# A second table of levels 1 to 8 for the key tiles one behind the diagonal, and no product of the high table in that level unit

## What is computed

```python
def _level_structure(t, num_levels):
    """level 0: s == t; level l>=1: t - s in [2^(l-1), 2^l). Clamped to num_levels-1."""
...
q = (x @ Wq.T).reshape(b, t, H, S); k = ...; v = ...            # H = 8, S = 128
g = -jax.nn.softplus(x @ Wg.T + bg)
lam = jax.nn.softplus((x @ Wdl.T).reshape(b, t, H, LV) + Lparam[None, None])   # LV = 12
G = jnp.cumsum(g, axis=1)
scores = jnp.einsum('bthd,bshd->bhts', q, k) * scale
decay = jnp.exp(jnp.where(mask, Gh[:, :, :, None] - Gh[:, :, None, :], -jnp.inf))
lamw = jnp.einsum('bthl,tsl->bhts', lam, lvl_oh)                # the weight of the level of t - s
y = jnp.einsum('bhts,bshd->bthd', scores * decay * lamw, v)
out = y @ Wo.T + x            # then a layer norm, a residual,
...                           # and a layer of 8 experts of which the best 2 are summed
```

## Time and profile before

| | before |
|---|---|
| three runs | 1454.74, 1455.56, 1457.22 us; median 1455.56 |
| span of the profiled execution, first to last instruction | 1454.1 us (no own time is given with it; it lies 0.6 below the lowest run) |
| busy: TensorE, VectorE, ScalarE, GpSimd | 95%, 72%, 81%, 64% of the span |
| mean granted TensorE clock | 0.991 of full speed |
| instructions | 30713, of them 10470 matmuls |
| transfer packets | 256341, 44.03 MB |

### The profile page before, as it was taken

One profiled execution on the slowest core, in us unless ns is written; L12 is line 12 of the kernel. 1 busy time (PEld: TensorE's weight loads), 2 busy tenths in 40 slices (PEclk: granted clock), 3 DMA queues, 4 the chain that ended last, 5 costly groups with the idle time before them and its releaser, 6 DMA issues.

```text
span 1454.1 us, 30713 instructions
## 1 busy us (share of the span) xinstructions
PE 1386.0 (95%) x10470; PEld 1169.2 (80%) x10470; DVE 1042.7 (72%) x2445; ACT 1171.0 (81%) x3412; POOL 926.3 (64%) x1018
## 2 busy tenths in 40 slices
PE   6899999999999999999999999999999999999997
PEld 5687888878888888878888788887888888878874
DVE  5766766787766976678766877668776697667677
ACT  3689889887788878898797977888878887888742
POOL 2354569755696467945588456875569655695573
PEclk9899999999999999999999999999999999999998
DMA  5311211102111122101121111110211011111100
GB/s 191 72 19 11 39 19 32 18 15 48 30 18 17 24 40 40 18 7 42 25 40 14 18 32 25 39 18 13 50 22 25 17 24 26 40 18 19 24 8 15
DMA packets 256341, 44.03 MB, mean 30 GB/s; under 512 B 197960, under 2 KB 254522, under 8 KB 256058
## 3 DMA queue, kind: packets, MB, share of 16 engines
q1 hardware_dynamic: 253980, 41.69, 15.1%
q10 hardware_dynamic: 2206, 0.40, 0.2%
HBM read 32.31 MB, written 9.18 MB: 29 GB/s over the span
## 4 chain that ended last, share of the span: by engine, by line
PE 58%; POOL 20%; ACT 12%; DVE 6%; issue 2%; DMA 1%; ACTq 0%; POOLq 0%; SPq 0%; DVEq 0%
PE o_ps L1427 16%; POOL a_lo L616 9%; PE l_ps L1364 7%; PE s_ps L1343 6%; ACT w_all L769 5%; PE s_ps L1345 5%; PE s_ps L1344 5%; PE aux L1343 5%; PE aux L1345 4%; PE aux L1344 4%; ACT a_hi L791 2%; POOL e_rs L622 2%; POOL late L641 2%; DVE a_all L988 1%; ACT L769 1%
## 5 line engine op out<-in xcount | busy, mean ns | idle before, releaser
L616 POOL TENSOR_TENSOR a_lo<-a_all,a_hi 128x512 fp32r<-128x512 f32 (+2 forms) x640 | 711.7, 1130 | 472.8 <-ACT a_hi L791 471.9
L769 ACT ACTIVATE w_all<-l_ps,bias 128x128 f32<-128x128 f32 x2287 | 627.6, 392 | 56.8 <-PE l_ps L1364 53.3
L988 DVE TENSOR_TENSOR a_all<-s_ps,w_all 128x512 f32<-128x512 f32 (+3 forms) x768 | 420.3, 553 | 241.2 <-PE s_ps L1345 205.2
L1427 PE MATMUL o_ps<-a_hi,v_all 128*128 128x512 f32 (+2 forms) x1280 | 467.8, 371 | 3.4 <-POOL a_lo L616 2.9
L791 ACT ACTIVATE a_hi<-a_all 128x512 fp32r<-128x512 f32 (+2 forms) x640 | 365.5, 595 | 116.3 <-DVE a_all L988 113.2
L1427 PEld LDWEIGHTS o_ps<-a_hi,v_all 128*128 128x128 f32 x1280 | 241.3, 188 | 36.7 <-POOL a_lo L616 7.5
L1343 PE MATMUL s_ps<-q_hi,xt_hi 128*128 128x512 f32 (+2 forms) x640 | 259.4, 405 | 5.9 <-DVE a_all L988 5.9
L1345 PE MATMUL s_ps<-q_hi,xt_lo 128*128 128x512 f32 (+2 forms) x640 | 231.1, 361 | 0.0
L1344 PE MATMUL s_ps<-q_lo,xt_hi 128*128 128x512 f32 (+2 forms) x640 | 230.3, 360 | 0.0
L1427 PE MATMUL o_ps<-a_lo,v_all 128*128 128x512 f32 (+2 forms) x640 | 230.0, 359 | 0.0
L1364 PE MATMUL l_ps<-rb,mask 96*128 96x64 f16 (+1 forms) x1774 | 143.7, 220 | 9.0 <-ACT w_all L769 8.8
(11 more groups left out here) (234 smaller groups left out, 2112.1 us busy)
## 6 DMA issues: line engine op xcount, KB each, us to landing
rb<-eb_scratch SPq DMA_DIRECT2D x1016, 0.8 KB
ra<-ea_scratch SPq DMA_DIRECT2D x508, 4.0 KB, 2.0
mt<-m_scratch SPq DMA_DIRECT2D x62, 128.0 KB, 2.1
nt<-n_scratch SPq DMA_DIRECT2D x62, 128.0 KB, 2.6
tx<-in_L_attn_x SPq DMA_DIRECT2D x9, 512.0 KB, 4.3
out<-late SPq DMA_DIRECT2D x15, 256.0 KB, 2.7
late<-in_L_attn_x SPq DMA_DIRECT2D x7, 512.0 KB, 4.2
ea_scratch<-tx SPq DMA_DIRECT2D x15, 128.0 KB
```

Of the source, the lines that this page charges most:

```text
L616: pool.tensor_tensor(a_lo[r][:, 0:t1 - t0], a[r][:, 0:t1 - t0], a_hi[r][:, 0:t1 - t0].bitcast(F32), ALU.subtract).then_inc(a_lo_done, 1)
L769: last = act.activation(w[k][:, W_AT[j] + dd, :].rearrange("p (f c) -> p f c", f=2), l_tiles[:, :, :, i - i0], ACT.Exp, bias=bias[b % 2][: ...
L988: dve.tensor_tensor(a[(n * NG + g) % NA][:, 0:t1 - t0], s_ps[:, g % 2, 0:t1 - t0], w[n % 2][:, at:at + (t1 - t0) // P, :].rearrange("p i n ...
L1427: last = pe.matmul(o, lhs[:, vr, j, :], rhs[r][:, 0:t1 - t0], start=fresh, stop=True, skip_group_check=True)
```

## The change

Unit 1 now takes a table of its own, rc, with the levels 1 to 8, so that its mask ma1 picks level 8 too and the 8 products with rb are gone from it (mask mb1 as well). For this ea_scratch holds nine levels a head instead of eight: ra is loaded from its rows 0 to 7, rc from rows 1 to 8, by 8 more transfers a head of the same shape. Level 8 is stored twice, in ea_scratch and in eb_scratch. The wait for rb goes from unit 1 to unit 2, and unit 1 waits for rc.

```diff
-    put("ma1", (s > t_a) & (level(P + t_a - s) == l_a))
+    put("ma1", level(P + t_a - s) == l_a + 1)
...
-    for d in (1, 2, 4):
+    for d in (2, 4):
         put(f"mb{d}", level(d * P + t_b - s) == l_b)
...
-NA_ROWS = LOW * H
-NE_ROWS = NLV * H
+N_LEV = NLV * H
+NA_ROWS = (LOW + 1) * H
+NB_AT = 96
+NE_ROWS = NB_AT + HIGH * H
...
+        rc = [sb(f"rc{k}", [P, NTA, TA, NC], F16) for k in range(2)]
...
+        def load_low(eng, n, qs, tables, first, landed):
+            b, h = divmod(n, H)
+            at = h * (LOW + 1) + first
+            for q in qs:
+                eng.dma_start(tables[n % 2][q * 2 * LOW:(q + 1) * 2 * LOW, :, q, :],
+                              ea_dram[b, at:at + LOW, :, q * T // TA:(q + 1) * T // TA]
+                              .rearrange("l r (t i) -> (l r) t i", i=NC)).then_inc(landed[n % 2], 16)
...
                     load_ra(sp, n, range(TA))
+                    load_rc(sp, n, range(TA))
                     load_rb(sp, n, range(TB))
...
                 load_ra(sp, 0, range(TA // 2))
+                load_rc(sp, 0, range(TA // 2))
                 load_rb(sp, 0, range(HALF_B, TB))
                 load_ra(sp, 1, range(TA))
+                load_rc(sp, 1, range(TA))
                 load_x(1)
...
                     pool.memset(rb[k][:, :, :, :], 0.0).then_inc(zeroed, 1)
+                    pool.memset(rc[k][:, :, :, :], 0.0).then_inc(zeroed, 1)
...
                     if u == 1:
+                        pe.wait_ge(rc_in[k], RA_IN * (n // 2 + 1))
+                    if u == 2:
                         pe.wait_ge(rb_in[k], RB_IN * (n // 2 + 1))
...
-                                          ra[k][:, tb, :, i0:i0 + cnt])
-                        if d in (1, 2, 4):
+                                          (ra, rc)[d][k][:, tb, :, i0:i0 + cnt])
+                        if d in (2, 4):
```

More of the change, by code:

```diff
@@ L70 @@
 _at = 0
-for _name, _n in (("ma0", NTA * P), ("ma1", NTA * P), ("mb1", NTB * P), ("mb2", NTB * P), ("mb4", NTB * P),
+for _name, _n in (("ma0", NTA * P), ("ma1", NTA * P), ("mb2", NTB * P), ("mb4", NTB * P),
                   ("m9", P), ("m10", P), ("ident", P), ("tri", P), ("suf", P), ("first", E), ("off", TA)):
@@ L124, in program @@
     n_dram = nc.dram_tensor("n_scratch", [H // 2, P, 2, 2, P], F32, kind="Internal").ap()
-    ea_dram = nc.dram_tensor("ea_scratch", [B, H * LOW, 2, T], F16, kind="Internal").ap()
+    ea_dram = nc.dram_tensor("ea_scratch", [B, H * (LOW + 1), 2, T], F16, kind="Internal").ap()
     eb_dram = nc.dram_tensor("eb_scratch", [B, H * HIGH, 2, T], F16, kind="Internal").ap()
@@ L298, in main_stage @@
         t_sh, e_sh1, e_sh2 = (sb(f"{k}_sh", [P, NC]) for k in ("t", "e1", "e2"))
-        z = sb("z", [P, NC, NLOG])
+        z_all = sb("z", [P, NC, NE_ROWS])
+        z = z_all[:, :, 0:NLOG]
         lz = sb("lz", [P, NC, NLOG])
@@ L351, in main_stage @@
         s_cat, s_rows, s_fwg, s_wes, s_wetc = (sem(n) for n in ("s_cat", "s_rows", "s_fwg", "s_wes", "s_wetc"))
-        ra_in, rb_in, m_in = ([sem(f"{n}{k}") for k in range(2)] for n in ("ra_in", "rb_in", "m_in"))
+        ra_in, rb_in, rc_in, m_in = ([sem(f"{n}{k}") for k in range(2)] for n in ("ra_in", "rb_in", "rc_in", "m_in"))
         l_mm, w_done, zeroed = sem("l_mm"), sem("w_done"), sem("zeroed")
@@ L415, in store_el_part, with load_rc @@
             eng.dma_start(ea_dram[b, :, part], src[0:NA_ROWS, :]).then_inc(t["stored"], 16)
-            eng.dma_start(eb_dram[b, :, part], src[NA_ROWS:NE_ROWS, :]).then_inc(t["stored"], 16)
-        def load_ra(eng, n, qs):
[L419 to L423, removed]
+            eng.dma_start(eb_dram[b, :, part], src[NB_AT:NE_ROWS, :]).then_inc(t["stored"], 16)
+        def load_low(eng, n, qs, tables, first, landed):
[5 more added lines that the diff above has]
+                              .rearrange("l r (t i) -> (l r) t i", i=NC)).then_inc(landed[n % 2], 16)
+        def load_ra(eng, n, qs):
+            load_low(eng, n, qs, ra, 0, ra_in)
+        def load_rc(eng, n, qs):
+            load_low(eng, n, qs, rc, 1, rc_in)
         def load_rb(eng, n, qs):
@@ L430, in load_rb @@
                               .rearrange("l r (t i) -> (l r) t i", i=NC)).then_inc(rb_in[n % 2], 16)
-        EL_ROWS = ((0, NA_ROWS, TA), (NA_ROWS, NE_ROWS, TB))
+        EL_ROWS = ((0, NA_ROWS, TA), (NB_AT, NE_ROWS, TB))
         def l_region(n, u):
@@ L568, in _ @@
                 sp.wait_ge(t["stored"], EL)
-                sp.wait_ge(zeroed, 4)
+                sp.wait_ge(zeroed, 6)
                 load_ra(sp, 0, range(TA // 2))
+                load_rc(sp, 0, range(TA // 2))
                 load_rb(sp, 0, range(HALF_B, TB))
                 load_ra(sp, 1, range(TA))
+                load_rc(sp, 1, range(TA))
                 load_x(1)
@@ L815, in level_ln @@
                     act.wait_ge(t["lamc"], b + 1)
-                    act.activation(lz[:, :, 0:NE_ROWS], z[:, :, 0:NE_ROWS], ACT.Ln).then_inc(t["lnl"], 1)
+                    act.activation(lz[:, :, 0:N_LEV], z[:, :, 0:N_LEV], ACT.Ln).then_inc(t["lnl"], 1)
                 def level_high(b, f):
@@ L911, in _ @@
                 act.wait_ge(t["stored"], EL)
-                act.wait_ge(zeroed, 4)
+                act.wait_ge(zeroed, 6)
                 load_ra(act, 0, range(TA // 2, TA))
+                load_rc(act, 0, range(TA // 2, TA))
                 load_rb(act, 0, range(HALF_B))
@@ L1031, in guard @@
                     dve.tensor_scalar(gd[:, :, :], z[:, :, LV * H:NLOG], -1.0, None, ALU.mult).then_inc(t["g"], 1)
-                    dve.tensor_scalar(z[:, :, 0:NE_ROWS], z[:, :, 0:NE_ROWS], 1e-19, None, ALU.max).then_inc(t["lamc"], 1)
+                    dve.tensor_scalar(z[:, :, 0:N_LEV], z[:, :, 0:N_LEV], 1e-19, None, ALU.max).then_inc(t["lamc"], 1)
                 by_head = sums[:, :, :, :].rearrange("p k i h -> p k h i")
@@ L1060, in level_logs @@
                     dve.wait_ge(t["run"], b + 1)
-                    for l0, l1, at in ((0, LOW, 0), (LOW, NLV, NA_ROWS)):
+                    for l0, l1, at in ((0, LOW + 1, 0), (LOW, NLV, NB_AT)):
                         n_l = l1 - l0
-                        dve.tensor_tensor(z[:, i0:i0 + HC, at:at + n_l * H].rearrange("p i (h l) -> p i l h", h=H),
+                        dve.tensor_tensor(z_all[:, i0:i0 + HC, at:at + n_l * H].rearrange("p i (h l) -> p i l h", h=H),
                                           lz[:, i0:i0 + HC, l0 * H:l1 * H].rearrange("p i (l h) -> p i l h", h=H),
@@ L1495, in turn_logs @@
                     for i in range(HC):
-                        last = pe.transpose(o[0:NE_ROWS, i * P:(i + 1) * P], z[:, f * HC + i, 0:NE_ROWS], c("ident"))
+                        last = pe.transpose(o[0:NE_ROWS, i * P:(i + 1) * P], z_all[:, f * HC + i, 0:NE_ROWS], c("ident"))
                     last.then_inc(aux_full, 1)
```

## The result

The changed kernel is slower: 1459.95 us in the median of 7 runs (1458.15 to 1460.88), against 1455.8 for the kernel before (7 runs, 1453.83 to 1457.66). The ratio is 1.0026, with a 95% interval of 1.0015 to 1.0036: 4 us, small but clear of none. Forecast were 1445.0 us and a range of 1436 to 1453.

The account below looks back on a forecast made before the run. TensorE was taken to bound most of each batch, GpSimd about two heads of eight. Matmuls saved 18.1 us, residual delay cost 6.0, start-up 1.5: -10.6 from 1455.56 gives 1445.0 us, forecast 1441 to 1449, range 1436 to 1453.

Parts of the forecast that it names:

- the second term: Batch boundaries: rc's issues on SP delay the residual that GpSimd's `shifted_x` waits for; 6 us lost, bounds 0 and 13.
- the 2 us that the prediction had named as a sign of being wrong: Batch boundaries: prediction wrong if GpSimd's idle time before `shifted_x` is absent or over 2 us.
- 1 us more at each of seven, 13: Upper bound of the residual's delay at the seven batch boundaries: 13 us in all.
- the shown: Batch boundary worked out from the profile rows around 557 to 577 us; `shifted_x` was to wait 0.6 us there.
- the first three chances: Forecast (1441 to 1449) 0.60, residual in time (1439.0 us) 0.15, TensorE the bound all over (1430.2 us) 0.05.
- SP's queue: Rival: rc issues cost more than ra's and everything behind them on SP slides; 1471 us at twice the price; chance 0.07.
- point of equality: Boundary stall at which that rival makes the change gain nothing: 2.4 us, when eight issues take 5.2 us instead of 3.74.
- The first term, the gain,: Unit 1 of each head: eight matmuls removed, 0.42 us each time, 43 on the chain; 18.1 us saved, bounds 12.2 and 26.9.
- others close the gap: Rival: in a batch's fourth and fifth head the saved time is waited away behind exponentials or VectorE; 1450.9 us; chance 0.13.
- GpSimd's stretch: 46 us around each batch boundary, about two heads of eight, where GpSimd has the last word and removed matmuls save 0.
- The start-up term: Start-up: twelve more issues ahead of head 1's rb on SP make TensorE stand still 1.5 us at unit 2; bounds 0, 3.

Follow-up runs that it names:

- the one with the gain alone: Kernel before with only the eight products of the high table left out of unit 1, no table, transfer or wait added: 1442.53 us, ratio 0.9911.

## Why the prediction was wrong

**The sum.** It was -18.1 + 6.0 + 1.5 = -10.6. Measured, term by term: -13, +16.3 (the heads of the six full batches and of the last, changed kernel against the one with the gain alone), +3, which makes +6; the traces say +5.0 and the medians +4. All three terms were off, in the same direction. The places were the right ones; what was mis-sized is told below, and in the largest, the residual, a second effect was missing.

**The step that failed** is the second term, "`late` is issued at 573.1 and lands at 577.3. `shifted_x` waits 0.6 us". It waited 2.7. I had SP's delay as 3.78 us and kept everything else as it was. Counted from the last unit of the head ahead, the residual was expected to land at 20.3 us and landed at 22.4. Of that, 0.5 us came on SP, where ra took 4.80 us at this place instead of 3.74 and rc 3.90 instead of 3.78, while nt, 1.19 instead of 1.90, gave 0.7 back; 0.3 was a pause before the issue; and 1.3 came because the landing took 5.5 us and not 4.2. None of the three is large. But the chain had 2.3 us of slack and a delay of 3 behind it, and a difference of two such numbers takes the whole error of both. The landing, the largest of the three, was the missing effect. SP, being late, no longer stood waiting for TensorE between the store and the residual, and in the runs the residual lands later where the two issues are close (the last section has the numbers; it is a pattern over the runs, and was not tested by itself). The waits at the seven boundaries were 1.6, 2.7, 2.7, 2.5, 1.2, 1.0 and 5.3 us, where 0, 1.15, 0.6, 0.6, 0.6, 0.6 and 2.1 had been forecast. Four are over the 2 us that the prediction had named as a sign of being wrong. Its bound of "1 us more at each of seven, 13" was too small too; 16.3 came. The sum of this term also had a slip: the first, the second, the shown and the last boundary leave three others and not four, so it gives 5.65 and not 6.2. And two thirds of 0.13 on top of the first three chances is 0.89, not 0.87. Neither changes the forecast.

**The rival that came true** is the last one, SP's queue, with a chance of 0.07. It came true in its outcome and not in its mechanism. I had tied it to an issue cost of 5.2 us for eight, which did not come (rc takes 3.9 in the median); landing and pauses did it instead. The stall was 17.0 / 7 = 2.4 us a boundary, the very number of its point of equality, but that is chance: at that stall the prediction had the kernel as fast as before, and it was 4 us slower, since with the gain and the start-up as measured, 13 and 3.1, equality lies at (13 - 3.1) / 7 = 1.4.

**The first term, the gain,** was counted from the chain: 43 units on it, 0.42 us each. 13 us is 31. The method overcounts, since being on the chain says that a unit ended last, not by how much. In head 5 unit 1 lies on the chain, and 0.35 of its 0.42 us are lost within 1.3 us, at a `scores` that waits for VectorE's `weigh`. That is the rival "others close the gap", but only half of it: head 4, which it named too, kept 0.35 us. Head 5 takes 2.2 us in the six full batches. Another 1.6 are missing in the first batch, where seven pieces saved 1.3 us and not 2.9; the rest of the 5 is not laid out. That the miss of 5 is near the 5.9 of the rival is in part luck. In the heads without a piece on the chain the count was nearly right: they gained 0.15, 0 and 0.

**GpSimd's stretch** was right for head 3 and shown by taking its load away. For head 2 it was wrong: GpSimd is nearly full there, and yet 1.4 us less of its work leaves the head as long as it was. That its wait for the residual goes fully into the time was right: a wait of 2.72 us made head 2 2.7 us longer.

**The start-up term**, 1.5, measured 3.1. The wait itself was sized well: rb landed at about 65.0 where 64.8 was forecast, and counted from unit 0 of that head, unit 2 starts after 9.4 us instead of 7.9, which is 1.5 more. The other 1.5 is lost behind it: from unit 2 to unit 3, over the same matmuls, it is 4.3 us instead of 2.7. That is TensorE's clock. In the busy times the granted clock is the third number from the right; first 60 to 64 us in the kernel before, then 60 to 68 in the changed one, and then its unit 2:

```profile
60.00:64.00 4.00, 4.00 (x19) 3.00 (x17) 1.78 (x4) 2.99 (x9) 2.14 (x7) 0.57 0.36 48
```

```profile
60.00:64.00 4.00, 1.44 (x7) 0.83 (x5) 1.67 (x4) 2.39 (x7) 2.83 (x10) 1.00 0.23 43
64.00:68.00 4.00, 2.96 (x15) 2.67 (x16) 0.69 (x1) 1.71 (x7) 3.65 (x4) 0.65 0.41 102
```

```profile
65.04 0.73 PE L1382 MATMUL l_ps<-rb,mask 96*128 96x96 f16 x8 [3.60 <-DMA rb<-eb_scratch]
```

In the kernel before, the clock is low ahead of unit 2 (0.52 from 60 to 62) and full behind it, from 64 on. In the changed kernel it is full ahead of it, so that TensorE is there at 61.4 and not at 63.3, and falls behind the wait of 3.6 us, to 0.50 from 66 to 68. The same fall, and the same 4.3 us, come behind waits of 3.9 us in the two experiments that keep the changed kernel's start-up (rc behind the residual, and the residual ahead of the store); where rb comes in time, there is no fall and it is 2.7. So the prediction lacked a step: here the wait cost 1.5 us of clock behind it as well. That the clock was low ahead of the unit in the row of before was in part an accident: in two of the six profiled executions that have the start-up of the kernel before it stayed at 1.00 there, and head 0 took 16.05 and 16.45 us instead of 17.7 to 17.95.

**The rule that the prediction weighed**, of the Trainium skill, page "DMA: Bandwidth & Descriptors", section "Issuing engines are not separate DMA queues", says that the sequencer's time is usually small beside the transfer. In this trace it is not small: one issue of this form takes 0.47 us beside a landing of 2.0, and the eight take 3.7 to 3.9, on a queue that had 26 issues already. That delay, with what followed from it, cost 16 us at the boundaries. The prediction went by the row, which was the right choice, and stopped at the row's own size.

## What to carry to other kernels

In this kernel the work added to SP's in-order queue cost nothing in most heads and was paid at the few places where something behind it was wanted soon. Find those places, and either put the new work behind it or count its slack against every part of the new delay, landing included, with their spread and not their median. A slack that is the difference of two times of which each moves by a microsecond is no cover. And a piece on the chain that ended last is worth its whole length only if the next longest chain is that much shorter: look at what waits within the next microseconds.

## What the runs showed that I had not expected

The residual's landing grew from 4.0 to 5.0 us to 5.1 to 5.9, though rc has been issued before it by then and nothing new follows it. With the store behind it it was 4.7 to 5.5, with rc behind it 4.2 to 5.5. Over all the profiled kernels it goes with the distance to the issue ahead of it on SP. Where the residual is issued within 0.8 us of the start of that issue, it lands in 5.2 us in the median (32 landings, 4.4 to 5.9); where it is issued 1.4 us or more behind, in 4.2 (31 landings, 3.8 to 5.4, one of them above 4.9). Kernels without rc show both. In the kernel before, the distance was never under 1.0 us, since SP stood waiting for TensorE there; in the changed kernel it is 0.65 at six of seven. That makes the later landing a likely consequence of SP's delay; no run set the distance by itself, and why a close neighbour should matter is open.

Leaving out 2.0 us of GpSimd's work in each batch is worth 12 to 15 us, as much as the removed products by themselves; where to put that work was not tried.
